# A transformer layer on one NeuronCore: the order of work in the opening, with attention units taken in pairs

## The reference, cut to what matters

```python
def _L0_attn_ref(x, qkv_w, out_w):
    qkv = (x @ qkv_w.T).reshape(B, S, 3, HEADS, HEAD_DIM)      # B = 8, S = 512
    q, k, v = jnp.transpose(qkv, (2, 0, 3, 1, 4))
    q = q * cos + rotate_half(q) * sin
    k = k * cos + rotate_half(k) * sin
    # mask: j <= i, and (same block of 64, or i or j among the first 4, or i - j <= 128)
    scores = jnp.einsum('bhqd,bhkd->bhqk', q, k) * scale
    attn = softmax(where(mask, scores, min), axis=-1)
    out = einsum('bhqk,bhkd->bhqd', attn, v)
    return out.transpose(...).reshape(B, S, E) @ out_w.T
def _L0_ffn_ref(x, ...):
    h = silu(tlin(x, w1)) * tlin(x, w2)                        # 256 -> 1024, weights -1, 0 or 1 times a scale
    h = gelu(tlin(h, h1)); h = gelu(tlin(h, h2))               # 1024 -> 1024
    return tlin(h, w3)                                         # 1024 -> 256
x = x + _L0_attn_ref(_layernorm(x), ...)
x = x + _L0_ffn_ref(_layernorm(x), ...)
```

## Time and profile before

| | |
|---|---|
| median of three runs | 1101.81 us |
| the profiled execution | 1101.9 us |
| its span, first to last instruction | 1100.1 us |
| PE busy | 1066.2 us (97%) |
| ACT, DVE, GpSimd busy | 720.7, 633.9, 459.5 us |
| the opening with all before it, until the first gated tile | 110.7 us |

### The profile page before, as it was taken

One profiled execution on the slowest core, in us unless ns is written; L12 is line 12 of the kernel. 1 busy time (PEld: TensorE's weight loads), 2 busy tenths in 40 slices (PEclk: granted clock), 3 DMA queues, 4 the chain that ended last, 5 costly groups with the idle time before them and its releaser, 6 DMA issues.

```text
span 1100.1 us, 21643 instructions
## 1 busy us (share of the span) xinstructions
PE 1066.2 (97%) x7602; PEld 875.8 (80%) x7602; DVE 633.9 (58%) x1988; ACT 720.7 (66%) x1776; POOL 459.5 (42%) x652
## 2 busy tenths in 40 slices
PE   5778999999999999999999999999999999999998
PEld 3446977889788987889778897788978898888887
DVE  5774656555665556655676555655666554555322
ACT  4874767756769559586586675875676855966422
POOL 5541535324634336254282353622554332423433
PEclk9798999999999999999999999999999999999999
DMA  8966459565473555554565545736546365432540
GB/s 320 336 231 203 161 157 296 174 193 172 157 212 102 183 172 189 176 155 135 171 222 155 160 168 153 234 101 207 163 152 205 94 195 172 125 107 66 185 134 21
DMA packets 112797, 190.16 MB, mean 173 GB/s; under 512 B 7216, under 2 KB 66864, under 8 KB 111664
## 3 DMA queue, kind: packets, MB, share of 16 engines
q1 hardware_dynamic: 112256, 182.45, 52.3%
q10 hardware_dynamic: 432, 6.29, 1.3%
HBM read 150.97 MB, written 45.09 MB: 178 GB/s over the span
## 4 chain that ended last, share of the span: by engine, by line
PE 88%; ACT 7%; DVE 3%; issue 1%; POOL 0%; DMA 0%; ACTq 0%; DVEq 0%; POOLq 0%
PE bank L772 39%; PE bank L742 11%; PE bank L799 6%; PE bank L676 5%; PE bank L545 5%; PE bank L642 4%; PE bank L612 4%; PE bank L650 4%; PE bank L576 2%; PE bank L701 2%; ACT Sm L939 2%; ACT a_act L959 1%; ACT a_hi L960 1%; PE bank L689 1%; PE bank L685 1%
## 5 line engine op out<-in xcount | busy, mean ns | idle before, releaser
L939 ACT ACTIVATE Sm<-Sm,smin 128x260 f32<-128x260 f32 (+2 forms) x512 | 241.3, 473 | 164.1 <-DVE smin L1135 163.8
L772 PE MATMUL bank<-b_hi,W 128*128 128x512 f32 x512 | 214.2, 418 | 0.2 <-POOL b_lo L1413 0.2
L772 PE MATMUL bank<-a_hi,W 128*128 128x512 f32 x512 | 208.5, 407 | 0.1
L772 PE MATMUL bank<-b_lo,W 128*128 128x512 f32 x512 | 201.7, 394 | 0.0
L772 PE MATMUL bank<-a_lo,W 128*128 128x512 f32 x512 | 201.0, 393 | 0.0
L1150 DVE COPY PT<-bank 128x512 f32<-128x512 f32 x128 | 87.8, 686 | 128.8 <-PE bank L676 118.6
L742 PE MATMUL bank<-x_hi,W 128*128 128x256 f32 x512 | 124.9, 286 | 0.0
L742 PE MATMUL bank<-x_lo,W 128*128 128x256 f32 x512 | 123.4, 283 | 0.0
L1422 POOL TENSOR_TENSOR a_lo<-a_act,a_hi 128x256 fp32r<-128x256 f32 x128 | 94.0, 738 | 62.2 <-ACT a_hi L990 62.1
L1135 DVE CUSTOM_DVE_ANT_0 Sm<-bank,msk,gmin 128x256 f32<-128x256 f32 x256 | 108.2, 479 | 11.0 <-PE bank L629 5.6
L772 PEld LDWEIGHTS bank<-b_hi,W 128*128 128x128 f32 x512 | 96.4, 188 | 18.2 <-issue 2.8
(11 more groups left out here) (120 smaller groups left out, 2193.6 us busy)
## 6 DMA issues: line engine op xcount, KB each, us to landing
W<-w_scratch SPq DMA_DIRECT2D x168, 512.0 KB, 4.0
qk_scratch<-split SPq DMA_DIRECT2D x56, 512.0 KB, 4.0
Qs<-qk_scratch SPq DMA_DIRECT2D x112, 128.0 KB, 4.3
Ks<-qk_scratch SPq DMA_DIRECT2D x14, 1024.0 KB, 9.2
w_scratch<-in_ffn_w SPq DMA_DIRECT2D x22, 512.0 KB, 6.9
x_in<-in_x SPq DMA_DIRECT2D x8, 512.0 KB, 7.6
stage_a<-in_ffn_w ACTq DMA_DIRECT2D x2, 2048.0 KB, 11.2
x<-in_x SPq DMA_DIRECT2D x8, 512.0 KB, 3.9
```

What stands on the lines that cost most here:

```text
L772: mm = nc.tensor.matmul(bank[n % 2][:, :], lhsT.bitcast(F32) if general else lhsT, rhs, start=(kk == 0 and part == 0), stop=(kk == NH - 1 ...
L939: ex = nc.scalar.activation(row, row, ACT.Exp, bias=smin[:, r, c:c + 1], scale=-1.0, accum_out=rowsum[:, i % 2, col:col + 1])
```

## The change

Only the opening changes. On DVE, an even step takes the minima of both its units, with the copy of turned values between them, and an odd step none; the residual goes ahead of the minima; LayerNorm statistics and normalisation of sequence 1, and the low halves of its splits, are placed by another count (the first two one step earlier, the low halves one later). On PE, the global scores and the values of the first keys of sequence 0 come one step later. On ACT, the high halves of the splits go behind the exponentials of their step; the look that stood ahead of the steps and the one at step 0 go to steps, and all LOOK_STEPS change. On GpSimd, the inverse roots for sequence 1 come one step earlier, and the second masking of queries goes ahead of the last rotary addition.

```diff
--- before.py
+++ after.py
@@ -61,7 +61,7 @@


 SHIFT, KNOWN = 3, UNITS
-LOOK_STEPS = (1, 3, 5, 7, 9, 11, 12)
+LOOK_STEPS = (1, 2, 3, 5, 7, 9, 10, 11, 13)
 MASKED_RING = 4
 DOWN_BANKS = (2, 3, 0, 1)
 DOWN_LATE = NH - 2
@@ -870,9 +870,9 @@
                 qk_projection(-2, n)
             v_projection(-2)
             for n in range(KNOWN):
-                if n == 2:
+                if n == 3:
                     global_scores(-2)
-                if n == 3:
+                if n == 4:
                     values_of_first(-2)
                 if n == KNOWN - 1:
                     pe.wait_ge(low_found, 1)
@@ -1007,7 +1007,7 @@
                     nq = n if r >= 0 else n - SHIFT
                     if with_q and nq - 1 in LN1_STEPS:
                         keep_xnT(r, nq - 1 - LN1_STEPS[0])
-                    if with_q and 0 <= nq - QK_STEP - 2 < 2 * NF:
+                    if r >= 0 and with_q and 0 <= nq - QK_STEP - 2 < 2 * NF:
                         split_hi(r, nq - QK_STEP - 2)
                     if with_f and n in (NH, 2 * NH):
                         gelu(r, n // NH - 1, 3)
@@ -1030,10 +1030,10 @@
                         gelu(r, n // NH, 1)
                     if with_f and n % NH == 7 and n < 2 * NH:
                         gelu(r, n // NH, 2)
+                    if r == -1 and 0 <= nq - QK_STEP - 2 < 2 * NF:
+                        split_hi(r, nq - QK_STEP - 2)
                     if r == -1 and n in LOOK_STEPS:
-                        check_weights(4 + LOOK_STEPS.index(n))
-                    if r == -1 and n == 0:
-                        check_weights(3)
+                        check_weights(2 + LOOK_STEPS.index(n))
                 if with_q:
                     keep_v(r)

@@ -1047,7 +1047,6 @@
             check_weights(0)
             check_weights(1)
             keep_v(-2)
-            check_weights(2)
             beside_attention(-1)
             act.wait_ge(attn_loaded, 16 * N_CONST)
             for r in range(NB):
@@ -1240,13 +1239,18 @@
                             keep_heads(a, i)
                         if n == UNITS + 1:
                             inverse_sums(a, NT - 1)
-                        if n < UNITS:
+                        if r < 0 and (i := tile_at(n, 8)) is not None:
+                            residual(a, i)
+                        if n < UNITS and (r >= 0 or n % 2 == 0):
                             masked_min(a, n)
                         if 0 <= n - T_LAG < UNITS:
                             keep_cur(a, n - T_LAG)
+                        if r < 0 and n < UNITS and n % 2 == 0:
+
+                            masked_min(a, n + 1)
                         if n < UNITS and (i := tile_at(n, 5)) is not None:
                             inverse_sums(a, i)
-                        if (i := tile_at(n, 8)) is not None:
+                        if r >= 0 and (i := tile_at(n, 8)) is not None:
                             residual(a, i)
                         if with_f and n == DEEP:
                             last_lo(r)
@@ -1258,24 +1262,24 @@
                             keep_x2lo(a, n - UNITS - 1)
                     if with_f and 0 <= n - DEEP - 1 < NT:
                         finish_y(r, n - DEEP - 1)
+                    if r == -1 and n == 2:
+                        keep_global_scores(0)
+                        take_global_min(0)
                     if with_q:
-                        if nq == 0:
+                        if nq == -int(r < 0):
                             for t in range(NT):
                                 ln1_stats(b, t)
-                        if nq == 1:
+                        if nq == 1 - int(r < 0):
                             for t in range(NT):
                                 ln1_apply(b, t)
-                        if 0 <= nq - QK_STEP - 2 < 2 * NF:
-                            split_lo(b, nq - QK_STEP - 2)
+                        if 0 <= nq - QK_STEP - 2 - int(r < 0) < 2 * NF:
+                            split_lo(b, nq - QK_STEP - 2 - int(r < 0))
                         if nq == KG_STEP:
                             global_keys(b)
                         if n == UNITS:
                             take_global_min(b)
                     if r == -1 and n == 1:
                         global_keys(0)
-                    if r == -1 and n == 2:
-                        keep_global_scores(0)
-                        take_global_min(0)
                     if r == -1 and n == 3:
                         keep_vg(0)
                     if r == -1 and n == KNOWN - 1:
@@ -1451,7 +1455,7 @@
                                 ln2_apply(a, i)
                         if r == -1 and n in (14, 15):
                             ln2_apply(a, n - 14)
-                    if with_q and nq == 0:
+                    if with_q and nq == -int(r < 0):
                         ln1(b)
                     if with_q and nq == QK_STEP:
                         spread_first(b)
@@ -1483,8 +1487,8 @@
             rotary(0, 1)
             mask_queries(0)
             rotary(0, 2)
+            mask_queries(1)
             rotary(0, 3)
-            mask_queries(1)
             beside_attention(-1)
             for r in range(NB):
                 gated(r)
```

## The result

The changed kernel took 1095.54 us (median of 5 runs, 1094.43 to 1095.61) beside 1101.76 for the kernel before in the same session, 6.2 us less; ratio 0.995, interval 0.9935 to 0.9966. The forecast was 1098.5 with a range from 1096.0: right in direction, but the gain is almost twice the one forecast, and the time lies half a microsecond under the range.

A forecast was written before the change was run, and what follows sets the result against it. Only the opening can pay, where in-order PE waits on DVE's minima, the score-bank ring and the shared bank. Terms 1.3 + 0.65 + 0.75 + 0 + 0.7 = 3.4 us, taken as 3.3, gave 1098.5 us, range 1096.0 to 1101.2.

The forecast's parts named there:

- A: Front of the opening, up to sequence 1's first query projection: earlier statistics, paired minima, moved look and global products; 1.3 us gained.
- A's lower value: Front: the last normalisation may lose up to about 0.8 us to GpSimd's mask and cast, so 1.0 us remains.
- B: Output projection of tile 0: second minimum goes ahead of the rotary, 1.4 us off DVE, 0.65 seen by PE.
- C: PE's third projection: residual ahead of the minima removes its 0.77 us wait, +0.75 us.
- D: Steps 9 to 13, looks in a row on ACT: neither gain nor loss, taken 0, bounds -1.9 to +0.6 us.
- Nothing new on SP: Among the items priced at nothing: SP, where saves shift with the later staging of second weights, gets no new cost.
- E: Tail of the opening: minimum 15 away from the flag, +0.3, and residual of tile 2 ahead of the copy, +0.4.
- R1: Rival: the clock helps too, the opening's first low stretch doesn't come, about 2.5 us more, 1096.0; chance 0.14.
- the forecast's own signs of being wrong: Gated tile later than 109, a low-clock stretch new or gone, or a pair's second turn waiting for DVE.
- R2: Rival: one short low stretch more between 59.5 and 83 us, costing about half of 3.3 us, 1100.2; chance 0.13.
- R3: Rival: ACT takes over early, with A and D both at their lower bounds, 1.2 us left, 1100.6; chance 0.15.
- R4: Rival: slower, clock low from third query projection to scores of unit 12, +7.3 us, 1105.8; chance 0.08.

The follow-up runs named there:

- kernels with fillers: Identity transposes nobody reads put into PE's gaps: about 85 in the old kernel, 1096.75 us; about 70 in the changed kernel, 1093.86 us.
- pairing alone: Old kernel with only the minima of two units paired on DVE, residual behind the second minimum of its pair: 1099.76 us.
- the residual alone: Old kernel with only the residual moved ahead of the minima: 1100.87 us.

## Why the prediction was right and wrong

**A, the front: near in size, wrong in cause.** 0.8 came for the 1.3 taken. The step that failed is "the normalisation ends at about 35.2 ... and ACT may copy the first half of xnT at 39.0". It does (35.65 and 39.45), but with the normalisation put back the copy comes at 40.01 from a start 0.6 later: ACT's queue set it. I gave the gain to the edit whose time I was following and didn't ask which of the two inputs of the copy came last. DVE and GpSimd do hold each other up: the copy of the global minima takes 0.90 us beside GpSimd's cast where it took 0.32, as the Trainium skill (SBUF — State Buffer, "Who interferes with whom") has it; but the normalisations don't meet it (the first three take 1.22 us and the last waits 0.27 for its root, where all four took 2.13). The 0.8 us by which A's lower value allowed for it didn't come, and the copy is hidden.

**B: right.** 0.65 forecast, 1.5 - 0.8 = 0.7 in the trace; the wait at the output projection is now 1.43 us, held by PE's own second projection.

**C: the mechanism right, the term mis-sized, 0.75 for 2.4.** The 0.77 us wait is gone as said; 0.9 in the scores and 0.7 in the turns and weighted values behind them came from the clock, which was low there before and isn't now. I had priced the stretch as it stood.

**D: right.** The looks in a row cost nothing; the lead is 3.9 before and 3.9 behind. ACT has one gap of 0.28 us between 65.7 and 82.9, on a saved split and not on the looks. That gap is the small end of a wait that the forecast didn't have ("Nothing new on SP"): neighbours of this kernel have 1.6 to 2.5 us of it.

**E: mis-sized, 0.7 for 4.0, most of it the clock.** The lead grows from 3.9 to 5.2 ahead of the flag, falls to 4.0 at its matmul, and grows to 5.7 behind the branch and 7.9 at the transposes. The first 1.3 is the low stretch that lasts from 80.5 to 84 where it lasted from 83 to 90; no term stood for it. "Minimum 15 no longer stands between the last heads and the flag ...: +0.3" had the right size nearly, by cancelling: 1.7 us are gone behind the flag's matmul, and 1.13 of them come back as a wait ahead of it, which leaves 0.5. The other term, "the transposes at 100.05 needn't wait ...: +0.4", was too small: with the turns' wait for ACT it is 1.2. The last 0.9 is the low stretch at 97, which was taken as given and which went with the gap. 1.3 + 0.5 + 1.2 + 0.9 = 3.9 of the 4.0.

**The sum and the rivals.** In the two traces the waits give 0.8 + 0.7 + 0.8 + 0.5 + 1.2 = 4.0 us of the 7.9 (A as it stands, with what clock is in it) and the clock 1.6 in C and 2.2 in E. Over the executions the change is worth 3.8 at equal clock by the line and 2.9 by the kernels with fillers (4.8 with the price of 0.21); the sum said 3.3 to 3.4. So the waits were walked about right in sum, and the step that failed is the clock, which the sum had at nothing. It was a rival, R1, 2.5 us for a first stretch that doesn't come. What happened is of that kind, the waits and the clock on top, though by other stretches: the mean low time fell from 24 to 17.5 us, worth 2.2 by the line and 1.4 at the fillers' price, and the profiled execution shows 10.5 us less. The chance of 0.14 looks too low, and treating the clock as an independent draw was the fault, though no simple rule replaces it: pairing alone took the mean low time to 20.5 us, the residual alone, which also takes a wait from PE, to 25.5. Two of the forecast's own signs of being wrong came true, low stretches new and gone, and a second turn of a pair that waits for DVE (1.41 us at 38.10). R2 came true once (the stretch at 70), outweighed; R3 and R4 didn't come. The fillers show the direction best: the granted clock of the old kernel goes from 0.988 to 1.000 and its time down by 4.9 us, with only fillers and their waits put in. The Trainium skill (TensorE: Matmul & The Clock Gate, "What's actually happening") says that activity releases the throttle; I had used the sentence for R4 alone. By that rule a wait of PE can cost more than its length, and the fillers agree.

## What to carry to other kernels

When PE waits in gaps of a microsecond or two, price each gap that an edit removes at its length plus what a low stretch behind it adds (here 0.34 us for each us of low clock by the line, 0.14 to 0.21 by the fillers), and compare kernels by executions together with their granted clock. Before following an edit along the chain, ask at each meeting point which input came last: the normalisation here ended 4 us earlier (35.65 for 39.73) for nothing. When an edit takes work out from behind a serial point, such as a flag read before a branch, ask whether it now stands ahead of it: 1.7 us gained there were 0.5 net. And time reorderings together as well as alone: two of them gave 3.9 us at equal clock where one alone gave 0.0 and 1.1.

## What was not expected of the hardware

One and the same program spreads by 8 us (1097.3 to 1105.7) on one core, and its mean granted clock, 0.985 to 0.994, goes with four fifths of it. Some 85 transposes whose result nobody reads brought the old kernel's clock to 1.000 and its time down by 4.9 us. And the last store lands either about 2.5 or 4.2 to 4.9 us behind the start of the last addition; what decides stays open, and it can hide 1.7 us of a gain in a single profile.
